# A fused cross-attention product and SwiGLU block on one core: new places for ctx quads, column sums, statistics and weight work, and VectorE quantising the first four row tiles

## What is computed

```python
def fake_quant(x, scale, zp):
    q = jnp.clip(jnp.round(x / s + z), 0.0, 255.0)
    return (q - z) * s

x = x + jnp.matmul(fake_quant(_layernorm(x)), fake_quant(ctx))
# second layer, on h = _layernorm(x) in bfloat16
qg, sg = _dynamic_quant(h, inv_gate)
qu, su = _dynamic_quant(h, inv_up)
inter = silu(qg @ w_gate.T * sg * s_wgate) * (qu @ w_up.T * su * s_wup)
inter = clip(inter, -10, 10).astype(bfloat16)
qi, si = _dynamic_quant(inter, inv_inter)
x = x + qi @ w_down.T * si * s_wdown
```

## Time and profile before

| | us |
|---|---|
| median of 3 runs | 1057.41 |
| lowest and highest | 1052.74, 1057.65 |
| the profiled execution, device time | 1058.52 |
| its span in the trace | 1056.8 |
| PE busy in the span | 939.6 (89%) |
| DVE, ACT, POOL busy | 666.1, 360.4, 295.3 |

### The profile page before, as it was taken

The page is one execution under the profiler, slowest core; times in us unless marked ns, Lnnn a source line. Parts: engine busy times, 40 slices in busy tenths (PEclk is TensorE's granted clock), DMA queues, the critical chain, the costliest instruction groups (busy, mean ns, idle before and its releaser), DMA issues.

```text
span 1056.8 us, 11253 instructions
## 1 busy us (share of the span) xinstructions
PE 939.6 (89%) x4192; PEld 416.0 (39%) x4192; DVE 666.1 (63%) x1006; ACT 360.4 (34%) x281; POOL 295.3 (28%) x256
## 2 busy tenths in 40 slices
PE   1689886799696778899999999999959989999998
PEld 1333332344242333344444444444424434444443
DVE  5469374657396777666777777777566694444443
ACT  4735456456445652222222333333226520000000
POOL 2226655364356021333333323223420000000000
PEclk9799988899897888899999999999989989999999
DMA  9665797976848803231333333333349630994112
GB/s 356 240 268 199 245 368 227 350 271 204 289 165 274 282 21 78 79 71 54 89 90 90 90 90 90 90 90 90 80 125 336 255 110 1 314 347 136 80 80 79
DMA packets 131686, 179.52 MB, mean 170 GB/s; under 512 B 111024, under 2 KB 111024, under 8 KB 113968
## 3 DMA queue, kind: packets, MB, share of 16 engines
q1 hardware_dynamic: 126848, 144.72, 43.8%
q10 hardware_dynamic: 4752, 34.08, 8.1%
q0 software_dynamic: 32, 0.00, 0.1%
HBM read 113.77 MB, written 37.75 MB: 143 GB/s over the span
## 4 chain that ended last, share of the span: by engine, by line
PE 58%; DVE 12%; issue 10%; DMA 8%; POOL 5%; ACT 5%; ACTq 0%; SPq 0%; DVEq 0%; POOLq 0%
PE ps L1099 36%; PE ps L1111 19%; DVE w_slots L849 5%; POOL x_tile L691 3%; PE ps L1079 3%; DMA ctx_stage<-in_ctx 2%; DVE small_operands L789 2%; DMA q1T<-x_q 2%; ACT x_i L462 1%; DMA w_raw<-in_w_gu 1%; DMA x_tile<-in_x 1%; DMA w_raw<-in_w_dn 1%; DVE ctx_u L762 1%; POOL ctx_slot L698 1%; DMA qT_odd<-q_f 1%
## 5 line engine op out<-in xcount | busy, mean ns | idle before, releaser
L1079 PE MATMUL ps<-ctx_slot,q1T 128*128 128x512 f16 x1024 | 237.2, 394 | 22.5 <-DMA q1T<-x_q 11.1
L1099 PE MATMUL ps<-w_slots,qT_even 128*128 128x512 f16 x1024 | 233.5, 391 | 21.1 <-issue 8.6
L1099 PE MATMUL ps<-w_slots,qT_odd 128*128 128x512 f16 x1024 | 231.9, 389 | 21.8 <-issue 19.7
L1111 PE MATMUL ps<-w_slots,qiT 128*128 128x512 f16 x1024 | 224.1, 382 | 4.1 <-DVE gate_and_up L891 4.1
L1079 PEld LDWEIGHTS ps<-ctx_slot,q1T 128*128 128x128 f16 x1024 | 102.7, 101 | 154.4 <-issue 16.8
L1099 PEld LDWEIGHTS ps<-w_slots,qT_even 128*128 128x128 f16 x1024 | 102.0, 100 | 151.8 <-issue 32.2
L1099 PEld LDWEIGHTS ps<-w_slots,qT_odd 128*128 128x128 f16 x1024 | 101.8, 100 | 151.2 <-issue 35.2
L1111 PEld LDWEIGHTS ps<-w_slots,qiT 128*128 128x128 f16 x1024 | 100.8, 99 | 127.3 <-DVE w_slots L849 4.6
L529 ACT ACTIVATE q_f<-q_i 128x2048 f16<-128x2048 int8 x32 | 61.1, 1910 | 195.0 <-DVE q_i L861 190.1
L920 DVE SCALAR_TENSOR_TENSOR down_tmp<-ps,small_operands,down_scales_b 128x512 f32<-128x512 f32 x64 | 48.0, 750 | 99.3 <-PE ps L1111 99.2
L870 DVE TENSOR_REDUCE small_operands<-x_and_xs 128x1 f32<-128x2048 f32 x19 | 43.4, 2284 | 105.9 <-POOL x_and_xs L672 102.3
(11 more groups left out here) (91 smaller groups left out, 679.1 us busy)
## 6 DMA issues: line engine op xcount, KB each, us to landing
ctx_stage<-in_ctx ACTq DMA_DIRECT2D x32, 1024.0 KB, 8.1
x_scratch<-x_tile SPq DMA_DIRECT2D x16, 1024.0 KB, 5.0
w_raw<-in_w_gu SPq DMA_DIRECT2D x16, 1024.0 KB, 9.1
x_tile<-x_scratch SPq DMA_DIRECT2D x16, 1024.0 KB, 8.4
x_tile<-in_x SPq DMA_DIRECT2D x15, 1024.0 KB, 9.4
x_and_xs<-x_scratch SPq DMA_DIRECT2D x15, 1024.0 KB, 5.8
out_x<-x_tile SPq DMA_DIRECT2D x15, 1024.0 KB, 5.1
w_raw<-in_w_dn SPq DMA_DIRECT2D x8, 1024.0 KB, 9.2
```

Source lines behind the costliest of these rows:

```text
L1079: last = nc.tensor.matmul(ps[:, bank(g), :], q1T[m][:, k, :], ctx_s[j % 4][:, k, :], start=(k == 0), stop=(k == KT - 1))
L1099: last = nc.tensor.matmul(ps[:, bank(S2 + i), :], qT[t % 2][:, which, k, :], wsl[:, unit(p, k // 4), hl, k % 4, :], start=(k == 0 and hl = ...
L1111: last = nc.tensor.matmul(ps[:, bank(S3 + i), :], qiT[t % 8][:, k, :], wsl[:, unit(4 + c, k // 4), hl, k % 4, :], start=(k == 0 and hl == ...
```

## The change

The tables of stage 1 are rewritten. `quads_at` names several quads for one g, and pulls quads 5 to 15 forward from g 1 to 11 to g 0 to 7; quads 16 to 31 go to g 20 to 35 without the gap at g = 31. DVE now takes quads ahead of adds. The first column sums and biases move one to three groups forward, those of chunks 4 to 7 two groups back, with all adds of a chunk later than before. Statistics of tiles 8 to 11 move one group back, those of tile 15 two groups forward. DVE does the int8 quantisation of tiles 0 to 3 in place of ACT (a new `quantise_x` in DVE's list; the other lines are in the diff). The weight work of part 0 on ACT and DVE starts one group earlier. In stage 2, SP issues two more weight loads of part 3 ahead of the transposition of tile 1's gate rows; ACT mixes part 3's `w_abs` with part 2's `w_hi`; DVE does part 3's scale ahead of an evacuation and the statistics of tile 2 between low halves of part 3.

```diff
+        quads_at = {0: (5,), 1: (6,), 2: (7, 8), 3: (9, 10), 4: (11, 12), 5: (13,), 6: (14,), 7: (15,)}
+        quads_at.update({g: (g - 4,) for g in range(20, 36)})
-        stats_at = {... 21: 8, 23: 9, 25: 10, 27: 11, 38: 12, 40: 13, 42: 14, 50: 15}
+        stats_at = {... 22: 8, 24: 9, 26: 10, 28: 11, 38: 12, 40: 13, 42: 14, 48: 15}
-        colsum_after = {6: 0, 9: 1, 11: 2, 14: 3, 25: 4, 29: 5, 33: 6, 37: 7}
+        colsum_after = {5: 0, 7: 1, 9: 2, 11: 3, 27: 4, 31: 5, 35: 6, 39: 7}
...
             load_w(3, 0)
-            transpose_q(0, 1)
-            for m, g in ((13, 2), (14, 3), (15, 1)):
+            for m, g in ((13, 2), (14, 3)):
                 sp.wait_ge(x2_stored[m % 8], 32)
                 load_w(3, g)
+            transpose_q(0, 1)
+            sp.wait_ge(x2_stored[15 % 8], 32)
+            load_w(3, 1)
...
+            def quantise_x(m):
+                dve.wait_ge(ln_ready, m + 1)
+                if m >= 1:
+                    dve.wait_ge(xq_ready, m)
+                nc.vector.tensor_scalar(xi8[:, :], X[m][:, :], a1[:, m:m + 1], b1[:, m:m + 1], ALU.mult,
+                                        ALU.add).then_inc(x_quantised, 1)
...
-                if g == 44:
+                if g == 43:
                     w_scale(0)
-                if 45 <= g < 49:
-                    w_lo(0, g - 45)
+                if 44 <= g < 48:
+                    w_lo(0, g - 44)
...
             w_abs(3, 0)
-            for g in range(4):
-                w_hi(2, g)
+            w_hi(2, 0)
+            w_hi(2, 1)
             w_abs(3, 1)
+            w_hi(2, 2)
             w_abs(3, 2)
+            w_hi(2, 3)
             w_abs(3, 3)
```

More of the change, by code:

```diff
@@ L458, in quantise_x @@
             def quantise_x(m):
-                act.wait_ge(ln_ready, m + 1)
-                if m >= 1:
+                if m >= 4:
+                    act.wait_ge(ln_ready, m + 1)
                     act.wait_ge(xq_ready, m)
-                nc.scalar.activation(xi8[:, :], X[m][:, :], ACT.Identity, bias=b1[:, m:m + 1],
-                                     scale=a1[:, m:m + 1]).then_inc(x_quantised, 1)
+                    nc.scalar.activation(xi8[:, :], X[m][:, :], ACT.Identity, bias=b1[:, m:m + 1],
+                                         scale=a1[:, m:m + 1]).then_inc(x_quantised, 1)
                 act.wait_ge(x_quantised, m + 1)
@@ L554, in _ @@
             cast_quad(4)
-            quantise_x(3)
             for g in range(G1):
-                if g in quad_at and g:
-                    cast_quad(quad_at[g])
+                if g == 0:
+                    quantise_x(3)
+                for q in quads_at.get(g, ()):
+                    cast_quad(q)
                 if g in colbias_at:
@@ L706, in _ @@
             for g in range(G1):
-                if quad_at.get(g, 0) % 4 == 3:
-                    cast_last_quad(quad_at[g] // 4)
+                for q in quads_at.get(g, ()):
+                    if q % 4 == 3:
+                        cast_last_quad(q // 4)
                 if g in stats_at:
@@ L937, in _ @@
             turn_out(1)
+            ln1_stats(3)
+            quantise_x(2)
+            quant_quad(4)
             for g in range(G1):
[L939 to L947 removed]
+                if g == 0:
+                    quantise_x(3)
+                if g in (1, 2):
+                    turn_out(g + 1)
+                for q in quads_at.get(g, ()):
+                    quant_quad(q)
+                for q in adds_at.get(g, ()):
+                    col_add(q)
                 if g in stats_at:
@@ L983, in _ @@
             w_lo(2, 3)
-            evac_up(1, 0)
             w_scale(3)
             sw_scale(3)
+            evac_up(1, 0)
+            w_lo(3, 0)
+            w_lo(3, 1)
             ln2_stats(2)
-            for g in range(4):
-                w_lo(3, g)
+            w_lo(3, 2)
+            w_lo(3, 3)
             evac_gate(0, 1)
```

29 lines of the change are left out of this document (10 added, 19 removed).

## The result

The changed kernel takes 1068.53 us (median; 1065.77 to 1069.99), where the kernel before took 1056.59 beside it: a ratio of 1.011, with a 95% interval of 1.0085 to 1.0134. Forecast was 1051.

A forecast was written before the change was run, and what follows sets the result against it. PE was taken as the bound, with stage 1 waits at column sums (21.9 us) and before tile 15 (8.06); -1.5 - 16.5 + 7.7 + 3.7 = -6.6 from 1058.52 or 1057.41 gave 1051 us, range 1039 to 1062.

The forecast's parts named there:

- The start: Early stage 1: DVE's quantisation gives a lead that early loads take away, leaving -1.5 us (-3.7 to +1.2).
- 3.2 us per quad at best: Early stage 1: the pace that ctx loads of 8.1 us, three buffers and a quantisation of 1.34 allow.
- new waits of 8 to 13: Early stage 1: us of new waiting at PE until the eleventh group, from late quads, adds and sums.
- the price of the shared port: Quantisations on DVE blocked by GpSimd would cost 3.8 us more for all four; left out of the sum.
- The middle: Later stage 1: quads ahead of adds and later sums bring the last ctx cast forward, -16.5 us (8.5 to 24).
- the ring: Quads 19 to 31: quad waits behind add, add for cast, cast for quad; quads first on DVE would open it.
- ACT's bound of 24: Middle: the most the last cast could gain, from ACT's 42.6 us of work after 145.89, against 212.60.
- PE's of 8.5 to 13.4: Middle: PE's gain in us if three waits of 18.1 go but the first sum keeps 4.7 to 9.6.
- no change: Rival, chance 0.15: transfers' pace limits the middle, waits only change owner; middle gives -8.5, time 1058.7 us.
- The hand-over: Before tile 15: low halves and scalars delay tile 11's last adjust, its store, and tile 15's transposition, +7.7 us (0 to 7.7).
- Early in stage 2: Two weight loads delay tile 1's transposition by 5.8 us, the new ACT order returns 2.1: +3.7 (-1.6 to +5.8).

The follow-up runs named there:

- q_only: The kernel before, with only the int8 quantisation of tiles 0 to 3 moved to DVE and what goes with it: 1049.7 us (0.9922).
- sq_undone: The changed kernel with quads 5 to 15 and the adds, sums and biases of chunks 0 to 3 back in their old places: 1057.6 us (0.9994).
- q_m_both: Kernel before plus quantisation on DVE, new middle, adds ahead of quads, loads of quads 22 and 23 held for tile 8's transposition: 1043.2 us (0.9877).
- h_later: The kernel before with part 0's high and low weight halves four groups later: 1058.8 us (1.0008).
- s_sums_undone: The changed kernel with column adds, sums and biases of chunks 0 to 3 back in their old places: 1070.1 us (1.0113).
- m_undone: The changed kernel with stage 1's middle as before (adds ahead of quads; adds, sums, biases, statistics in old places): 1073.0 us (1.0154).
- h_undone: The changed kernel with part 0's weight work and tile 15's statistics back in their old places: 1062.1 us (1.0046).

## Why the prediction was wrong, point by point

*The start, forecast -1.5, found +3.7.* The mechanism held: the loads of early quads take the lead away, and it lasts to the end where quads stay in their places (`q_only`, -7.4 in the span). The pace held too, 3.4 us per quad up to quad 12 against "3.2 us per quad at best", and so did the new waits of 8 to 13 up to the eleventh group, with 9.5 and 1.3. What was mis-sized is the rest of that sum. The fourth group starts at 46.33, 6.9 sooner than before and not 8.6: the row at 44.61 begins with half of the third group, and `sq_undone`, which has the quads in their old places, is at 43.43. Behind the wait of 9.5, 32 matmuls took 8.64 us where they later took 7.07, and the sum 1.89 instead of 1.03: 2.4 us, with a granted clock of 0.64 from 66.30 to 73.00 (0.50 is the level of 1.2 GHz, 1.00 that of 2.4), which the sum had at nothing. And the statistics of tile 4 start at 93.16 (forecast 83.6 to 88.6), 3.1 us behind the end of the eleventh group (90.08), because adds of chunk 3 (the last two at 88.92 and 91.61) stand ahead of them on DVE.

*The quantisation on DVE.* The four took 1.31 us in the mean, so leaving out the price of the shared port was right for them. It came out the other way for the adds, several of which now run beside POOL's adjusts (from 82.08 to 94.37): their mean went from 1.456 to 1.862 us. The Trainium skill, in "SBUF — State Buffer", section "Who interferes with whom", says that an instruction of VectorE with two SBUF inputs contends with a GpSimd one that reads SBUF; the rows agree, and no run here separates that cause from others.

*The middle, forecast -16.5, found +0.1 at group 40 (some -2 over all traces).* This is the step that decided the sign. The waits at the sums of chunks 4 to 6 came to 21.5 us (18.1 before, forecast under 10), and the last ctx cast to 217.47 (212.60 before, forecast near 196):

```profile
217.47 1.90 POOL L702 TENSOR_SCALAR ctx_slot<-ctx_u 128x2048 f16<-128x2048 uint8 x1 [7.36 <-ACT ctx_u L447]
```

The step that failed is "This opens the ring: the quad no longer waits behind the add". The order on DVE put quads that weren't loaded ahead of adds of the chunk before, which is the ring turned round and not opened; with adds first again, PE gains 6.5 by group 40. Neither bound held the second cause: tile 8's transposition, `x_q` and ACT's casts. ACT's bound of 24 counted work and no waits, and PE's of 8.5 to 13.4 let all waits but the first go. With both causes taken away (`q_m_both`) the middle gives PE 9.2 us, inside PE's bound and far from ACT's. The rival "no change" was right that the waits only change their owner. Its reason, the transfers' pace over the whole stretch, doesn't fit `q_m_both`, which moves the same data.

*The hand-over, forecast +7.7, found +8.7 (12.5 less 3.8).* The moves named are the right ones, and the size is in part luck. The evacuation of tile 11's last chunk came at 268.16 (260.12 before): 4.2 beyond the shift of 3.8, where 4.1 was forecast. The adjust came at 274.51 (260.94 before), another 5.5 later behind the scalars of tile 15, where 3.6 was forecast:

```profile
268.16 0.74 DVE L820 SCALAR_TENSOR_TENSOR x_tile<-ps,small_operands,x_tile 128x512 f32<-128x512 f32 x1
269.84 2.47 DVE L794 BATCH_NORM_STATS2 small_operands<-x_tile 128x6 f32<-128x512 f32 x4 [0.95 <-DMA x_tile<-in_x]
...
274.51 8.60 POOL L695 TENSOR_TENSOR x_tile<-x_tile,col_bias 128x512 f32<-128x512 f32 x7
...
276.22 6.16 SPq L273 DMA_DIRECT2D w_raw<-in_w_gu  x4
282.48 9.16 SPq L265 DMA_TRANSPOSE q1T<-x_q  x1
```

The loads of part 1 follow 12.6 later than before (263.62). But in the kernel before they didn't hold the transposition: it was issued at 274.37, 5.5 after the last of them (263.62 + 5.29), as soon as tile 15's own cast was done:

```profile
272.34 1.91 ACT L470 ACTIVATE x_q<-x_i 128x2048 f16<-128x2048 int8 x1
```

The prediction took SP's list alone for what held it. Of the 12.6, 8.1 reached the transposition, 4.3 beyond the shift. The other 4.4 come from its flight, 11.2 us right behind the four loads against 6.8 before, which the sum didn't hold. `h_later` agrees: its adjust came 2.5 sooner, and PE waited as long.

*Early in stage 2, forecast +3.7, found +3.0 (15.0 less 12.0).* Right in mechanism and size: the transposition costs ACT 10.24 us of waiting where it cost 4.95, and the new order gains 2 against it.

```profile
369.03 1.91 ACT L530 ACTIVATE q_f<-q_i 128x2048 f16<-128x2048 int8 x1 [10.24 <-DMA qT_odd<-q_f]
```

*Not in the sum, found -3.2 between groups 8 and 14 of stage 2.* Most of it is the clock. PE runs group 12 of stage 2 there after a pause (3.30 us before the change, 2.84 after), and in the kernel before the first 5 us of it were granted 0.50, the level of 1.2 GHz (13 matmuls), in the changed kernel 1.00, that of 2.4 GHz (22). This isn't the change's own: in this stretch `s_sums_undone`, `m_undone` and `h_undone`, with the changed stage 2, get back 0.1 to 0.4, and `q_m_both`, with stage 2 as before, 3.1. Window from:to, length, busy by engine, clock, DMA share, GB/s, first before, then after:

```profile
447.00:452.00 5.00, 5.00 (x13) 1.77 (x12) 4.76 (x9) 1.87 (x1) 0.00 (x0) 0.50 0.87 268
```

```profile
461.00:466.00 5.00, 4.68 (x22) 2.18 (x23) 4.79 (x9) 1.91 (x1) 0.00 (x0) 1.00 0.84 264
```

Together, 3.7 + 0.1 + 8.7 + 3.0 - 0.5 (from group 54 to stage 2) - 3.2 and -0.3 after that are the 11.5 us of the spans. The range ended too low because the middle's term was let down only to -8.5: with 0 in its place the prediction's own sum is +9.9, from 1057.4 to 1067.3. Its upper end was also added up wrongly: 1058.7 with the start's 2.7 and stage 2's 2.1 on top is 1063.5, not 1062, and still below the 1068.5 measured.

## What to carry to other kernels

In an engine's in-order list, a load-fed step that is moved forward doesn't wait alone: everything behind it waits for its transfer, so a table must not ask for more per group than the loads bring, which here was about one quad. A remedy that leaves the time as it was may still work where it is applied: adds first gave PE 6.5 us by group 40, and what followed hid most of them, so look at the starts of groups before a cause is called wrong. And a gain of one part can be hidden by losses elsewhere: the quantisation alone was worth 0.8%, and the change around it made 1.1% of loss.
